# Reordering the seams of an expert phase: combine between two turns, sends shared with VectorE, and a shorter start

## The reference

```python
logits = einsum('bgtd,des->bgtes', grouped, controller) + tie
perm = (logits == max(logits, axis=tokens of the group))      # one token per expert slot
dispatched = einsum('bgtd,bgtes->bgesd', grouped, perm)
inner = relu(einsum('bgesd,desf->bgesf', dispatched, f1) + bias)
intermediate = einsum('bgesf,esfd->bgesd', inner, f2)
out = einsum('bgesd,bgtes->bgtd', intermediate, perm)
x = layernorm(x + out)
```

## Time and profile before

| | us |
|---|---|
| median of 3 runs (2159.98 to 2168.12) | 2160.15 |
| the profiled execution | 2164.57 |
| its span, first to last instruction | 2162.8 |

### The profile page before, as it was taken

One profiled execution on the slowest core, in us unless ns is written; L12 is line 12 of the kernel. 1 busy time (PEld: TensorE's weight loads), 2 busy tenths in 40 slices (PEclk: granted clock), 3 DMA queues, 4 the chain that ended last, 5 costly groups with the idle time before them and its releaser, 6 DMA issues. The chain is left out here.

```text
span 2162.8 us, 43991 instructions
## 1 busy us (share of the span) xinstructions
PE 2001.3 (93%) x16950; PEld 1478.7 (68%) x16950; DVE 1439.3 (67%) x2836; ACT 1042.7 (48%) x1875; POOL 437.1 (20%) x282
## 2 busy tenths in 40 slices
PE   7999999999999889899987999999569988989888
PEld 6777777777777634344437888888458677677685
DVE  5878778787777735455546888888534655645645
ACT  4444444444444434444444555555222744826637
POOL 0100011000010024454445555555000000000000
PEclk9999999999999999999999999999759999999999
DMA  5133333334333368788867888777328476584663
GB/s 172 66 116 122 127 102 118 112 112 139 106 112 105 124 197 222 225 229 238 221 177 239 242 245 244 237 239 223 119 80 279 142 233 213 167 292 149 198 229 118
DMA packets 228340, 380.16 MB, mean 176 GB/s; under 512 B 23679, under 2 KB 90405, under 8 KB 228005
## 3 DMA queue, kind: packets, MB, share of 16 engines
q1 hardware_dynamic: 218917, 360.55, 53.5%
q10 hardware_dynamic: 9216, 16.78, 2.0%
HBM read 251.13 MB, written 126.12 MB: 174 GB/s over the span
## 5 line engine op out<-in xcount | busy, mean ns | idle before, releaser
L90 PE MATMUL p_pu<-p_xT_high,p_win_high 128*128 128x512 f32 (+1 forms) x816 | 329.9, 404 | 13.9 <-DVE p_win_low L85 11.8
L447 ACT ACTIVATE p_t<-p_pu,p_tbias,p_taps 128x512 f32<-128x512 f32 (+1 forms) x192 | 146.6, 764 | 357.9 <-PE p_pu L92 357.0
L91 PE MATMUL p_pu<-p_xT_high,p_win_low 128*128 128x512 f32 (+1 forms) x816 | 313.4, 384 | 0.0
L92 PE MATMUL p_pu<-p_xT_low,p_win_high 128*128 128x512 f32 (+1 forms) x816 | 313.0, 384 | 0.0
L1469 DVE COPY e_taken<-e_pun 128x1024 f32<-128x1024 f32 x128 | 156.7, 1224 | 161.3 <-PE e_pun L1395 95.0
L1469 ACT COPY e_taken<-e_pun 128x1024 f32<-128x1024 f32 x128 | 129.6, 1013 | 267.4 <-PE e_pun L1395 188.5
L564 DVE SCALAR_TENSOR_TENSOR p_t<-p_pu,p_taps,p_t 128x256 f32<-128x256 f32 (+1 forms) x384 | 208.4, 543 | 6.9
L849 POOL TENSOR_TENSOR q_y<-q_y 128x512 f32<-128x512 f32 x128 | 160.2, 1271 | 196.8 <-DVE q_y L870 196.8
L85 POOL TENSOR_TENSOR p_xT_low<-p_xT,p_xT_high 128x2048 fp32r<-128x2048 f32 (+1 forms) x16 | 71.3, 4455 | 617.9 <-ACT p_xT_high L80 617.9
L90 PEld LDWEIGHTS p_pu<-p_xT_high,p_win_high 128*128 128x128 f32 x816 | 155.4, 190 | 46.6 <-DVE p_xT_low L85 10.0
L92 PEld LDWEIGHTS p_pu<-p_xT_low,p_win_high 128*128 128x128 f32 x816 | 154.9, 190 | 32.8
(11 more groups left out here) (150 smaller groups left out, 3892.9 us busy)
## 6 DMA issues: line engine op xcount, KB each, us to landing
q_av<-s_SV SPq DMA_DIRECT2D x64, 512.0 KB, 4.3
s_Z<-q_z SPq DMA_DIRECT2D x128, 256.0 KB, 3.2
o_zin<-s_Z SPq DMA_DIRECT2D x64, 512.0 KB, 4.0
e_ff<-in_L_ffn_f SPq DMA_DIRECT2D x64, 512.0 KB, 5.0
e_it<-in_L_ffn_f SPq DMA_DIRECT2D x48, 512.0 KB, 4.7
s_X<-p_t SPq DMA_DIRECT2D x64, 256.0 KB, 2.3
s_SV<-k_shared SPq DMA_DIRECT2D x64, 256.0 KB, 2.0
s_SV<-p_sout SPq DMA_DIRECT2D x64, 256.0 KB, 2.0
```

What stands on the lines that cost most here:

```text
L90: pe.matmul(out, a[0], b[0], start=start, stop=False)
L91: pe.matmul(out, a[1], b[0], start=False, stop=False)
L92: return pe.matmul(out, a[0], b[1], start=False, stop=stop)
L447: nc.scalar.activation(t[r][m % 2][:, c], pu[(W + n) % 3][:, c], ACT.Identity, bias=tbias[:, w:w + 1], scale=taps[:, w, 2:3]).then_inc(t_o ...
```

## The change

- `ident` is loaded once, in the front phase, and handed to all; `top[1]` is kept as `late_top`.
- The output phase makes only two of the eight late choices (those over groups that chunk 0 needs). DVE makes the others in the experts phase, one instruction over 32 groups for each of chunks 1 to 3, in the middle of the quad stage before (`choose(c + 1)`); PE waits for `chosen_ok` before it transposes them.
- At the start of the experts phase SP issues the eight token tiles first; PE waits for no constants; DVE does the bias work (`prepare`) and the clearing of `pq` after chunk 0's sends.
- In chunk 0 the sends and picks use a fourth bank pair, the two `pq` banks.
- In a seam PE's order becomes turn, combine of the tile before, turn, dispatch. In the final seam it is turn, combine of the tile before, turn.
- In chunks 1 to 3 the second send of every second tile (m odd) is copied by DVE instead of ACT.
- ACT: copy of turn, copy of turn, root, perhaps copy of send, finish. DVE: add, moments, send, perhaps a second send, perhaps a pick, scale.

```diff
@@ output_phase @@
             if n == TILES + 3:
-                return range(UNITS, 2 * UNITS)
+                return range(UNITS, UNITS + UNITS // 4)
@@ experts_phase, numbered and bank pairs @@
                         yield "send", c, 2 * m - 2, ON_DVE
-                        yield "send", c, 2 * m - 1, ON_ACT
+                        yield "send", c, 2 * m - 1, (ON_ACT, ON_DVE)[m % 2 if c else 0]
...
+            ring = NU + 1 if c == 0 and kind in ("pick", "send") else NU
+            unit.append(u % ring)
+            before.append(last.get(u % ring))
+            last[u % ring] = u
...
-                if u >= NU:
-                    pe.wait_ge(taken_ok[taker[u - NU]], ONE + taken_by[u - NU])
-                return pun[u % NU]
+                if before[u] is not None:
+                    pe.wait_ge(taken_ok[taker[before[u]]], ONE + taken_by[before[u]])
+                return units[unit[u]]
@@ SP @@
-            sp.dma_start(ident[:], A["ident"]).then_inc(consts, 16)
+            for m in range(NX0):
+                load_x(0, m)
             sp.dma_start(side[:], A["side"]).then_inc(consts, 16)
-            for m in range(2):
-                load_x(0, m)
             sp.dma_start(bias[:], A["ffn_bias"]).then_inc(consts, 16)
-            for m in range(2, NX0):
-                load_x(0, m)
@@ PE @@
-            pe.wait_ge(consts, ONE + 48)
...
                     if c and m < TC:
                         turn(c - 1, 2 * m)
+                    if c and m:
+                        combine(c - 1, m - 1)
+                    if c and m < TC:
                         turn(c - 1, 2 * m + 1)
                     if c < CHUNKS and m:
                         dispatch(c, m - 1)
                         if m % PT == 1 and m < 3 * PT:
                             choices(c, m // PT + 1)
-                    if c and c < CHUNKS and m < TC:
-                        combine(c - 1, m)
-                    if c == CHUNKS and m:
-                        combine(c - 1, m - 1)
@@ ACT @@
-                behind = 1 if c < CHUNKS else 2
-                for m in range(TC + behind):
-                    j = (c - 1) * TC + m - behind
+                for m in range(TC + 1):
+                    j = (c - 1) * TC + m - 1
                     if c and m < TC:
                         take("turn", c - 1, 2 * m)
-                    if c and m >= behind:
-                        root(j)
                     if c and m < TC:
                         take("turn", c - 1, 2 * m + 1)
-                    if c and m >= behind:
-                        finish(j)
+                    if c and m:
+                        root(j)
                     if c < CHUNKS and m:
                         take("send", c, 2 * m - 1)
+                    if c and m:
+                        finish(j)
@@ DVE @@
+            def choose(c):
+                now = K[:].rearrange("p (n r t) -> p n r t", r=2, t=GT)[:, c * GP:(c + 1) * GP, 1, :]
+                best = late_top[:, c * GP:(c + 1) * GP].rearrange("p (n a) -> p n a", a=1)
+                dve.tensor_tensor(now, now, best.to_broadcast([P, GP, GT]), ALU.is_equal).then_inc(chosen_ok, 1)
...
-                for m in range(TC + behind):
-                    j = (c - 1) * TC + m - behind
-                    if c and m >= behind:
-                        scale(j)
+                for m in range(TC + 1):
+                    j = (c - 1) * TC + m - 1
+                    if c and m:
+                        add(j)
+                        if c < CHUNKS and m == TC:
+                            clear(c)
+                        moments(j)
+                    if c and m and m == TC:
+                        scale(j)
                     if c < CHUNKS and m:
                         take("send", c, 2 * m - 2)
+                        take("send", c, 2 * m - 1)
                         if m % PT == 1 and m < 3 * PT:
                             take("pick", c, m // PT + 1)
-                    if c and behind - 1 <= m < TC + behind - 1:
-                        add(j + 1)
-                        ...
-                        moments(j + 1)
+                    if c and m and m < TC:
+                        scale(j)
                 if c == CHUNKS:
                     break
+                if c == 0:
+                    prepare()
+                    clear(0)
                 for i in range(-2, Q, 2):
+                    if i == 2 * GT // 4 and c + 1 < CHUNKS:
+                        choose(c + 1)
```

More of the change, by code:

```diff
@@ L130, in output_tables @@
     return {"wout": [sb(f"wout_{n}", [P, DT, D], F32R) for n in ("high", "low")], "ctrl": sb("ctrl", [P, DT, ES]),
-            "ident": sb("ident", [P, P]), "grow": sb("grow", [P, DT, P]), "grow_c": sb("grow_c", [P, DT, N2]),
+            "grow": sb("grow", [P, DT, P]), "grow_c": sb("grow_c", [P, DT, N2]),
             "fbias": sb("fbias", [P, DT]), "bout": sb("bout", [P, D]), "eps": sb("eps", [P, 1]),
@@ L134, in output_tables, with front_phase @@
             "x0": [sb(f"x0{s}", [P, DT, P]) for s in range(AHEAD)], "x": [sb(f"x{s}", [P, D]) for s in range(AHEAD)]}
-def front_phase(nc, sem, A, S, K, F):
+def front_phase(nc, sem, A, S, K, ident, F):
     J = CH // N1
@@ L148, in ps @@
             return ctx.enter_context(nc.psum_tensor("p_" + name, shape, F32))
-        ident = sb("ident", [P, P])
         win_s = [sb(f"win_{n}", [P, DT, 3 * D], F32R) for n in ("high", "low")]
@@ L738, in _ @@
                     sp.dma_start(O["ctrl"][:], A["ffn_controller"].rearrange("(k p) e -> p k e", p=P)).then_inc(carried, 16)
-                    sp.dma_start(O["ident"][:], A["ident"]).then_inc(carried, 16)
-            sp.wait_ge(carried, ONE + 16 * 6)
+            sp.wait_ge(carried, ONE + 16 * 5)
             sp.wait_ge(tiles_in, ONE + 16 * 3 * AHEAD)
@@ L876, in _, with output_phase @@
                 multiply(p)
-def output_phase(nc, sem, A, S, K, O):
+def output_phase(nc, sem, A, S, K, ident, late_top, O):
     TILES = N2
@@ L891, in ps @@
             return ctx.enter_context(nc.psum_tensor("o_" + name, shape, F32))
-        ctrl, ident, grow, grow_c, fbias, bout, eps, wout_s = (O[n] for n in (
-            "ctrl", "ident", "grow", "grow_c", "fbias", "bout", "eps", "wout"))
+        ctrl, grow, grow_c, fbias, bout, eps, wout_s = (O[n] for n in (
+            "ctrl", "grow", "grow_c", "fbias", "bout", "eps", "wout"))
         zin = [sb(f"zin{s}", [P, 2, D]) for s in range(NZ)]
@@ L907, in output_phase @@
         logit = K[:].rearrange("p (n r t) -> p n r t", n=N1, r=2)
-        top = [sb(f"top{s}", [P, N1]) for s in range(2)]
+        top = [sb("top", [P, N1]), late_top]
         pc = [ps(f"pc{s}", [P, DT, P]) for s in range(2)]
@@ L1160, in _, with experts_phase @@
                     choose(u)
-def experts_phase(nc, sem, A, S, K):
+def experts_phase(nc, sem, A, S, K, ident, late_top):
     GC = 64
@@ L1179, in experts_phase @@
         rows = taken[:].rearrange("p (k b e g) -> p k b e g", k=DT, b=GP, e=ES)
-        ident, side, eps = sb("ident", [P, P]), sb("side", [P, 2]), sb("eps", [P, 1])
+        side, eps = sb("side", [P, 2]), sb("eps", [P, 1])
         bias, nbias, back = sb("bias", [P, Q]), sb("nbias", [P, Q]), sb("back", [P, Q, 4])
@@ L1192, in experts_phase @@
         pun = [ctx.enter_context(nc.psum_tensor(f"e_pun{s}", [P, 2, D], F32)) for s in range(NU)]
-        pq = [ctx.enter_context(nc.psum_tensor(f"e_pq{s}", [P, D], F32)) for s in range(2)]
+        pqs = ctx.enter_context(nc.psum_tensor("e_pq", [P, 2, D], F32))
+        pq = [pqs[:, s] for s in range(2)]
+        units = [p[:] for p in pun] + [pqs[:]]
         ph = [pq[s // 2][:, s % 2 * GP * 4:(s % 2 + 1) * GP * 4] for s in range(4)]
@@ L1226, in numbered @@
                         yield "quad", c, i, (ON_ACT, ON_DVE)[i % 2]
-        number, taker, taken_by = {}, [], []
+        number, taker, taken_by, unit, before, last = {}, [], [], [], [], {}
         for kind, c, i, on in numbered():
-            number[kind, c, i] = len(taker)
+            u = len(taker)
+            ring = NU + 1 if c == 0 and kind in ("pick", "send") else NU
+            number[kind, c, i] = u
+            unit.append(u % ring)
+            before.append(last.get(u % ring))
+            last[u % ring] = u
             taken_by.append(1 + taker.count(on))
@@ L1352, in choices @@
             def choices(c, b):
+                if c:
+                    pe.wait_ge(chosen_ok, ONE + c)
                 to = bank_pair(number["pick", c, b])[:, 0]
@@ L1454, in keep @@
             eng.wait_ge(u_ps, ONE + u + 1)
-            at = pun[u % NU][:]
+            at = units[unit[u]]
             if kind == "pick":
@@ L1512, in clear @@
                     dve.wait_ge(res_ok, ONE + c * TC)
+                else:
+                    u = last[NU]
+                    dve.wait_ge(taken_ok[taker[u]], ONE + taken_by[u])
                 for p in pq:
@@ L1550, in take, with prepare @@
                 keep(dve, dve.tensor_copy, ON_DVE, kind, c, n)
```

(29 more changed lines are left out.)

4 lines of the change are left out of this document (1 added, 3 removed).

## The result

The changed kernel takes 2193.74 us (median of 4 runs, 2186.05 to 2200.69), the kernel before 2162.78 in the same comparison; the ratio is 1.0139, 95% interval 1.0098 to 1.0181: slower by 31 us. 2184 was forecast, range 2168 to 2199.

The account below looks back on a forecast made before the run. PE, busy 93% of the span, was taken to bound the kernel. Start and seam 0 -30.7, first quad stage -4.5, seams 1 to 3 +51 and final seam +8.4 gave +24.2; from 2160.15 that is 2184 us, range 2168 to 2199.

Parts of the forecast that it names:

- Part 1: Output phase's end and start of seam 0: six choices go, -3.67; first dispatch at 1542.2 instead of 1551.10.
- Part 2: Seam 0 with four bank pairs: layer 1 starts at 1576.5 instead of 1607.18, -30.7 (ends -23 and -36.6).
- The 29: Seam 0, first to last dispatch: the middle between 23.1 at the higher clock and 35.6 at the lower.
- The 5.3: Seam 0, last dispatch to layer 1: last copies, bias work 2.12, clearing 0.55 and about 0.25 until PE starts.
- Part 3: First quad stage: should come near the second, -4.5 (ends -5.4 and -1); moved choices cost 0.
- Part 4: Seams 1 to 3: a new closed cycle makes each 17.0 longer, +51 in all (ends +45 and +56).
- The cycle: Seams 1 to 3: dispatch, DVE send, scale, ACT finish, next turn's copy, dispatch; 5.23 even, 6.37 odd, 6.97 with pick.
- the forecast's terms: Seams 1 to 3: dispatch to send 1.20, each DVE send 1.14, reciprocal to finish 0.45, to turn's copy 1.29, to dispatch 1.15.
- Part 5: Final seam: root, reciprocal and finish come behind both copies; 3.89 per tile instead of 3.29, +8.4 (ends +7 and +10).
- The clock rival: Seams 1 to 3: granted clock falls as PE idles, up to +105, 2289; a third of it 2219; chance 0.05.

Follow-up runs that it names:

- Experiment 6: The changed kernel with three bank pairs in chunk 0 as before, the rest of the new start kept: 2215.54 us, ratio 1.0239.
- experiment 1: The changed kernel with DVE running scale before the tile's sends in seams 1 to 3: 2145.34 us, ratio 0.9923.
- experiment 5: The changed kernel with ACT's finish a tile later in all seams, behind the next tile's two turn copies and ahead of root: 2137.29 us, ratio 0.9878.
- experiment 2: The changed kernel with all second sends copied by ACT again, scale still behind the sends: 2162.38 us, ratio 0.9992.
- experiment 3: The changed kernel with PE running turn, turn, combine, dispatch: 2189.08 us, ratio 1.0127.
- experiment 4: The changed kernel with the seam orders of the kernel before on PE, ACT and DVE, the new start kept: 2127.13 us, ratio 0.9838.
- experiment 7: The kernel with new start and old seam orders (2127), dispatch running one bank pair's eight matmuls, then the other's, two row groups at a time: 2138.09 us.

## Why the prediction was right

*Part 1.* Six choices fewer, from the start of `choose` to the phase's first issue 3.79 instead of 7.41: right at -3.6. From there to the first dispatch 2.59 (3.0 was put in). The -7.1 of the table also has the earlier phases in it, which ended 2.15 later in this execution (1537.60 against 1535.45). That it fell 1.8 short while part 2 gave 2.8 more is luck for the sum.

*Part 2.* Four pairs: first dispatch to layer 1 in 31.5, where 34.3 was the sum of 29 and 5.3. The 29 was the middle between two clock levels, not a forecast of when the clock rises. It rose about 1552: in the windows above PE is busy 3.64 of 4 and 2.00 of 2 us at 0.50, then 1.64 of 2 us at 0.88. The seam 0 of the other kernels with a fourth pair took 30.9 to 33.9. The 5.3 behind the last dispatch came as worked out, in the open: bias work from 1572.43, clearing at 1574.63, layer 1 at 1575.43. Experiment 6 shows that this part hangs on the fourth pair (56.2 without it).

*Part 3.* -3.1 instead of -4.5, inside its ends, but its reason is not borne out. It was that the first quad stage was long (67.8) because seam 0 before it left PE at its lower clock and little busy. In experiment 6 seam 0 is as long as before (56.2, clock 0.50 to 0.60, and 0.50 at its end), and the first quad stage takes 62.3, less than the 64.7 here. What made it 67.8 before stays open, and that the number fits is luck. The moved choices cost nothing, as forecast: one takes 1.21 in the quad stage, and DVE still waits 0.43 for PE behind it. Rows of the second quad stage:

```profile
1769.63 1.23 DVE L1471 COPY e_taken<-e_pun 128x1024 f32<-128x1024 f32 x1 [2.10 <-PE e_pun L1399]
1770.77 1.21 DVE L1570 TENSOR_TENSOR k_shared<-k_shared,k_top 128x1024 f32<-128x1024 f32 x1
1771.90 0.60 DVE L1526 SCALAR_TENSOR_TENSOR e_hid<-e_pq,e_nbias,e_back 128x128 f32<-128x128 f32 x2
1772.93 1.22 DVE L1471 COPY e_taken<-e_pun 128x1024 f32<-128x1024 f32 x1 [0.43 <-PE e_pun L1399]
```

*Part 4.* The cycle is shown from three sides: its intervals to 0.03 us, its links by removal (experiments 1 and 5 cut it in two places, 2 takes one link out of half the tiles), and what is outside it by an edit without effect (3). The chain above also has the forecast's terms one by one: 1.20, 2.28, 0.43, 1.28 and 1.16, against 1.20, 2.28, 0.45, 1.29 and 1.15. That moving the second send to DVE brings nothing while scale is behind it is shown too: undoing it took 9.0 a seam out of the intervals (experiment 2).

*Part 5.* 3.88 per tile (3.89 forecast), 68.0 for the final seam (68.2).

*What was off by size.* +29.9 between the two spans, +24.2 forecast: seams 2.2 more, three later quad stages 3.4 more, where 0 stood. The seams' share is the clock, told of next: without its 3.0 they are 16.7 to 16.8 longer each, where 17 was forecast. The later quad stages vary by more than that between the experiments (59.3 to 67.7), with the same code; their causes were not looked into. The distance between the medians, 31, has the spread of the runs in it.

*The clock rival* came true in small: in seam 1 two intervals were longer, 6.14 and 5.85 instead of 5.21, in seam 2 one (6.04), in seam 3 one (5.85). Each of the four begins with a dispatch for which PE had waited 1.86 or 1.87; in three of them this dispatch is itself slower (2.09, 2.02 and 1.40 instead of 1.17), in the fourth the turn behind it. The first, in timeline and windows:

```profile
1664.12 2.09 PE L1372 MATMUL e_pun<-e_picked,e_xt 32*128 32x128 f32 x32 [1.86 <-ACT e_it L1471]
```

```profile
1662.00:1664.00 2.00, 0.26 (x3) 0.07 (x1) 1.12 (x3) 1.53 (x3) 0.00 (x0) 1.00 0.32 120
1664.00:1666.00 2.00, 1.88 (x32) 1.82 (x32) 0.00 (x0) 1.08 (x2) 0.00 (x0) 0.53 0.06 19
```

The mean clock of seam 1 was 0.95, of the two others 0.98 and 0.97 (0.99 to 1.00 before). Twelve dispatches of the three seams had such a wait and four were followed by a longer interval; why these four, no row here tells. In experiment 2, where PE waits 0.69 to 0.74 before a dispatch, no interval is longer and the clock is 0.99 to 1.00: part of what experiment 2 wins is this. The page of the Trainium skill that I weighed ("TensorE: Matmul & The Clock Gate", section "A second HAM failure mode: psum-queue depth-cycling") is borne out as to its direction; here it is worth 0.6 to 1.6 us a seam, not the cost of the rival.

## What to carry to other kernels

When a small instruction is moved behind a large one, follow who waits for it, and in front of whom *that* one stands in its own queue; if the path returns to where it began within one iteration, an iteration can't take less than its sum, however idle the engines are. Here it took just that, since no engine's own work and no other such path was longer. Sum such cycles before moving work from a busy engine to a free one. And take a change apart: here one part was worth 35 us, and the orders beside it cost more than it gave (67 against 35).

## What was not expected of the hardware

Dispatch's matmuls on 32 rows by 128 columns take 1.10 us for a tile when four row groups take turns, and 1.65 when two groups at a time do (experiments 4 and 7): 34 and 52 ns per matmul of the trace's 32, with the same data and a granted clock of 1.00 in both. At the lower clock, on the first dispatch of seam 0, it is 2.09 against 3.10, in a place where no earlier copy is waited for. With two groups in turn the matmuls also write to two PSUM banks in turn instead of four; which of the two costs the time was not separated.
